# Quarter tiles for the key-value products, and one half of the values scaled by GpSimd instead of VectorE

## What is computed

```python
qkv = xf @ qkv_w.T + qkv_b                       # xf: B x N x C, N = 128*128 pixels, C = 64
qkv = qkv.reshape(B, N, HEADS, 3 * HEADC).transpose(0, 2, 1, 3)
q, k, v = jnp.split(qkv, 3, axis=-1)             # 8 heads of 8
k = _layernorm(k, kln_w, kln_b)                  # over the 8 of a head: (t - mean) / (std + eps)
v = _layernorm(v, vln_w, vln_b)
kv = jnp.einsum('bhnd,bhne->bhde', k, v) / N
av = jnp.einsum('bhnd,bhde->bhne', q, kv)
```

## Time and profile before

| | |
|---|---|
| median of 3 runs | 2723.24 us (2722.13 to 2723.75) |
| the profiled execution's own time | 2722.5 us |
| its span | 2720.6 us |
| TensorE busy, share of the span | 2563.4 us, 94% |
| VectorE | 1866.0 us, 69% |
| ScalarE | 1238.3 us, 46% |
| GpSimd | 159.3 us, 6% |
| share of the chain that ended last in the sweeps' products (L719) | 80% |
| key-value stage, first bias product to last Gram burst | 2456.35 to 2631.62 us |

### The profile page before, as it was taken

The page is one execution under the profiler, slowest core; times in us unless marked ns, Lnnn a source line. Parts: engine busy times, 40 slices in busy tenths (PEclk is TensorE's granted clock), DMA queues, the critical chain, the costliest instruction groups (busy, mean ns, idle before and its releaser), DMA issues.

```text
span 2720.6 us, 115694 instructions
## 1 busy us (share of the span) xinstructions
PE 2563.4 (94%) x45062; PEld 2447.6 (90%) x45062; DVE 1866.0 (69%) x6022; ACT 1238.3 (46%) x2502; POOL 159.3 (6%) x275
## 2 busy tenths in 40 slices
PE   2889999999999999997899999999999999959999
PEld 1279999999999999997899999999999999959973
DVE  7976666666566666678666666666666666777875
ACT  1656664222233333356666632222333334566768
POOL 1420000000000000000000000000000000003434
PEclk9999999999999999999899999999999999989989
DMA  6720001222400000023900012223000000240005
GB/s 259 179 73 0 0 0 32 62 60 60 104 0 0 0 5 0 0 62 103 373 22 0 0 39 62 61 60 96 0 0 0 0 0 0 77 108 2 3 14 235
DMA packets 158375, 146.46 MB, mean 54 GB/s; under 512 B 22497, under 2 KB 146018, under 8 KB 154210
## 3 DMA queue, kind: packets, MB, share of 16 engines
q1 hardware_dynamic: 146432, 142.65, 17.9%
q10 hardware_dynamic: 11874, 2.90, 0.5%
HBM read 61.61 MB, written 50.33 MB: 41 GB/s over the span
## 4 chain that ended last, share of the span: by engine, by line
PE 88%; DVE 3%; issue 3%; DMA 3%; ACT 2%; SPq 1%; ACTq 0%; POOL 0%; DVEq 0%
PE banks L719 80%; PE banks L773 4%; PE banks L785 1%; DVE state L915 1%; DMA state<-x_in 1%; PE banks L766 1%; ACT res L481 1%; PE banks L692 1%; DVE state L1023 1%; DMA res<-resid 1%; SPq L262 1%; DMA resid<-state 0%; ACT state L487 0%; POOL state L421 0%; DMA state<-turn_ring 0%
## 5 line engine op out<-in xcount | busy, mean ns | idle before, releaser
L719 PE MATMUL banks<-x_row,w_taps 128*64 128x124 f32 (+2 forms) x40640 | 2201.6, 270 | 14.4 <-DVE x_row L946 8.3
L719 PEld LDWEIGHTS banks<-x_row,w_taps 128*64 128x64 f32 x40640 | 2199.1, 135 | 16.7 <-DVE x_row L946 9.9
L946 DVE SCALAR_TENSOR_TENSOR x_row<-banks,sweep_nbias,biased_row 128x128 f32<-128x128 f32 x2032 | 713.2, 351 | 718.8 <-PE banks L719 702.9
L521 ACT ACTIVATE biased_row<-state,sweep_bias 128x256 f32 (+1 forms) x762 | 512.1, 673 | 1025.6 <-DVE state L949 589.2
L517 ACT ACTIVATE biased_row<-state,aff,gn_a 128x64 f32 (+1 forms) x1016 | 367.0, 432 | 179.3 <-DVE state L955 179.3
L949 DVE SCALAR_TENSOR_TENSOR state<-banks,sweep_nbias,biased_row 128x128 f32 (+1 forms) x1016 | 443.5, 437 | 0.1
L955 DVE SCALAR_TENSOR_TENSOR state<-banks,sweep_nbias,biased_row 128x64 f32 (+1 forms) x1016 | 237.2, 275 | 0.2
L955 DVE SCALAR_TENSOR_TENSOR turn_ring<-banks,sweep_nbias,biased_row 128x64 f32<-128x64 f32 x1016 | 237.3, 276 | 0.0
L407 POOL TENSOR_SCALAR res<-res 128x128 f32<-128x128 f32 x64 | 43.2, 675 | 2395.6 <-ACT res L630 2395.4
L692 PE MATMUL banks<-res,ffn_w 64*64 64x512 f32 x512 | 120.2, 611 | 11.6 <-DVE state L915 10.4
L773 PEld LDWEIGHTS banks<-kvw_s,state 64*128 64x128 f32 x1024 | 118.0, 308 | 0.1
(11 more groups left out here) (123 smaller groups left out, 780.4 us busy)
## 6 DMA issues: line engine op xcount, KB each, us to landing
state<-turn_ring SPq DMA_DIRECT2D x512, 64.0 KB, 1.9
state<-x_in SPq DMA_DIRECT2D x16, 1024.0 KB, 20.8
resid<-state SPq DMA_DIRECT2D x64, 256.0 KB, 3.7
res<-resid SPq DMA_DIRECT2D x16, 1024.0 KB, 8.9
res<-resid SPq DMA_DIRECT2D x32, 512.0 KB, 6.0
resid<-state SPq DMA_DIRECT2D x16, 1024.0 KB, 10.6
out_y<-state SPq DMA_DIRECT2D x16, 1024.0 KB, 3.9
state<-resid SPq DMA_DIRECT2D x32, 256.0 KB, 8.5
```

The source lines that it names most:

```text
L521: nc.scalar.activation(as_cells(n, biased_row[:, k, :, :]), cells(n, slice(0, B), i, k, g), ACT.Identity, bias=sweep_bias[:, n:n + 1]).the ...
L719: last = nc.tensor.matmul(out_ps[blk, :, lo:hi], w_taps[:, n % 2, s, blk], x_row[c][src][:, :, s + lo:s + hi], start=at == 0, stop=at == T ...
L946: nc.vector.scalar_tensor_tensor(x_row[c][par][:, :, 2:2 + HALF], ps, nb, br, ALU.max, ALU.add).then_inc(row_ready[c], 1)
```

## The change

Three things are changed, all in the key-value stage. The product of 128 pixels (weights of 128 columns) becomes two of 64 pixels, each to its half of the output partitions. VectorE's scaling takes only the four pixel groups of the even parity, 256 elements a partition. The four of the odd parity are scaled by GpSimd, in `scale_odd_pixels(n - 1)`, which stands behind `tails(n)`; the Gram product waits for both. Nothing is left out of the computation.

```diff
+        odd_v_scaled = sem("odd_v_scaled")
...
+        def values_and_scale(n, u):
+
+            by = rkv[:, n % KV_SLOTS, :].rearrange("p (u h) -> p u h", h=HEADS)[:, u, :]
+            return gram_kv[:, n % KV_SLOTS, u, 1, :, :], by.unsqueeze(3).to_broadcast([P, PARTS, HEADS, HD])
...
+            def scale_odd_pixels(n):
+
+                pool.wait_ge(inverse_ready, n + 1)
+                pool.wait_ge(kv_copied, n + 1)
+                v, by = values_and_scale(n, slice(PARTS, 2 * PARTS))
+                nc.gpsimd.tensor_tensor(v, v, by, ALU.mult).then_inc(odd_v_scaled, 1)
+
             for n in range(KV_TILES):
                 tails(n)
+                if n:
+                    scale_odd_pixels(n - 1)
+            scale_odd_pixels(KV_TILES - 1)
...
                         col = q * BANK + t * KVN
-                        last = nc.tensor.matmul(pair[n % KV_BANKS][:, col:col + KVN], half_rows[blk, top:top + P, b, w],
-                                                kvw_s[blk, b, :], start=False, stop=t == PARTS - 1)
+                        for m in range(2):
+                            at = slice(m * C, (m + 1) * C)
+                            last = nc.tensor.matmul(pair[n % KV_BANKS][at, col:col + KVN],
+                                                    half_rows[blk, top + m * C:top + (m + 1) * C, b, w],
+                                                    kvw_s[blk, b, :], start=False, stop=t == PARTS - 1)
                 last.then_inc(kv_done, 1)
...
                 pe.wait_ge(v_scaled, n + 1)
+                pe.wait_ge(odd_v_scaled, n + 1)
...
-                v = gram_kv[:, slot_, :, 1, :, :]
-                by = rkv[:, slot_, :].rearrange("p (u h) -> p u h", h=HEADS).unsqueeze(3).to_broadcast([P, 2 * PARTS, HEADS, HD])
+                v, by = values_and_scale(n, slice(0, PARTS))
                 nc.vector.tensor_tensor(v, v, by, ALU.mult).then_inc(v_scaled, 1)
```

## The result

The changed kernel takes **2700.53 us** (median of 4 runs, 2699.72 to 2701.83), the kernel before 2723.49 us in the same session (4 runs, 2722.13 to 2724.07). The ratio is 0.9917, 95% interval 0.9900 to 0.9934: 23 us faster. The forecast was 2694, its range 2679 to 2726. The profiled execution took 2700.32 us, its span is 2698.4 us, 22.2 less than before.

A forecast was written before the change was run, and what follows sets the result against it. TensorE was taken to bound the key-value stage at 2.677 us a tile; with GpSimd next at 2.13 + 0.05, 59 tiles save 29 us: 2722.5 becomes 2693.2, plus 0.7 for the median, 2694 us, range 2679 to 2726.

The forecast's parts named there:

- Part 1: Key-value products in quarter tiles: a group of four loads costs 0.11 us, eight 0.88, and TensorE's tile becomes 1.82 us.
- half-way case: Key-value loads partly take turns: 0.165 us a group, TensorE's tile 2.26, time 2699; counted within the forecast.
- Part 2: Next bound in the key-value stage: GpSimd at 2.13 us a tile, over VectorE's 1.91, TensorE's 1.82 and ScalarE's 1.79.
- P: Time of GpSimd's new scaling product of 256 elements, taken as 0.80 us; near 0.7 the sum would be below 35 us.
- Part 3: GpSimd's product and VectorE's scaling overlap: 0 to 0.27 us a tile, mostly in VectorE's spare 0.22; 0.05 taken.
- The new wait: The Gram products' wait for `odd_v_scaled` costs nothing as long as GpSimd's pace holds; about half a tile of slack.
- The start and the end as nothing: Before and behind the 59 tiles the change was taken as nothing: about 1 us each, of opposite sign.
- The loads take turns: Rival: strided loads of both column halves alternate, TensorE's tile stays at 2.70 us, time 2722 to 2726; chance 0.13.
- Exclusion: Rival: VectorE's 0.42 us scaling adds fully to GpSimd's tile, making 2.55; 7.5 us saved, 2716; chance 0.08.
- The clock: Rival: TensorE's clock falls to 1.2 GHz in the stage, tile near 3 us, 19 us slower, 2742; chance 0.03.
- P stayed far below 1.35: Rival: GpSimd's product is dear, deciding from 1.35 us; at 1.6 the kernel is 15 us slower, 2738; chance 0.06.
- The sum: Key-value stage: 2.677 - (2.13 + 0.05) = 0.50 us saved in each of 59 tiles, 29 us, 2693.2 profiled.

The follow-up runs named there:

- half_packed: Changed kernel, but the second column half's 64 weights are neighbouring elements of `state` (other pixels) while the first half stays strided; 2686.03 us.
- quarters_only: Changed kernel with the quarter products kept, but all scaling given back to VectorE and GpSimd's product and semaphore removed; 2699.02 us.
- packed_64: Changed kernel, quarters and split scaling kept, but each product's weights are 64 neighbouring elements of `state` (other pixels); 2686.82 us.
- packed_128_pool: Kernel before, with weights of 128 neighbouring elements of `state` (other pixels) and the scaling split between VectorE and GpSimd; 2683.31 us.

## Why the prediction was right and where it was off

**What bounds the kernel before: right.** TensorE's products set the stage's pace, and the gain came where it was looked for: 25.5 us in the 59 tiles on which the sum was made, less 3.3 ahead of them.

**Part 1, the group of four: the step that failed.** "If the two column halves read their weights side by side" a group was to be 0.11 us. It is 0.147 in the median (in one tile five groups in a row start at 2519.692, 2519.840, 2519.987, 2520.137 and 2520.288 in the single records, 0.149 apart): the rows of before showed a strided load beside a moving operand, and none showed two strided loads in one set of partitions. The argument that moving reads cost the loads nothing didn't carry over. half_packed shows the cost only where both are strided. So the products took 1.26 instead of 0.88, the first one stood 0.40 behind the bias product instead of 0.31, the Gram products took 0.58 instead of 0.63, and TensorE's tile was 2.24, not 1.82. The text had a half-way case, "0.165 a group, TensorE 2.26, 2699", and its time is what came, within 2 us. That it came so near is in part luck: with 0.147 a group the prediction's own terms give 0.63 + 0.31 + 1.18 = 2.12, below the 2.18 that it had for GpSimd. The other 0.12 are the 0.09 behind the bias product, which no row of before showed, and 0.08 by which the products take longer than eight groups, less 0.05 of the Gram products.

**Part 2, "GpSimd becomes the bound": wrong.** GpSimd idles in over 5 of 50 us in the changed kernel, and quarters_only has the same tile without its product. The estimate of its tile, 2.13, was too high as well: P was well placed as a sum (0.80 taken and 0.05 for the overlap; 0.83 to 0.89 measured in the means of the kernels, of which 0.63 are the product alone), but 0.16 for two more gaps and the 0.08 in the 1.33 were too much; three operations back to back have one gap of 0.09, 1.92 us in all. VectorE's 1.91 fits (packed_64's tile is 1.92 in the median, where TensorE has room), its scaling took 0.42 as in the earlier trace rows. By packed_64 and packed_128_pool, with products as short as Part 1 had them the time would have been near 2683 to 2687, not 2694: two errors of opposite sign, 0.42 us a tile too little for TensorE and over 0.2 too much for GpSimd, left the forecast only 6.5 us low. The number is near, then, but by luck and not by its mechanism: the engine that was named as the next bound was not the bound. (Its other sum, "below 35 us" with a P near 0.7, comes out at 35.2: 59 x (2.677 - 2.03 - 0.05).)

**Part 3, the overlap: right in kind, larger in size.** The product takes 0.63 alone and 0.83 to 0.89 with VectorE's scaling ahead of it, some 0.2 to 0.26 a tile instead of 0.05. In packed_128_pool and packed_64 it ends 0.91 us after the start of VectorE's scaling, whether it starts 0.045 us behind it (then it takes 0.867) or 0.092 (0.821): it loses what is left of the first 0.28 us of VectorE's 0.42, just as the prediction's 0.15 of free start would have it. What failed is the guess that GpSimd would lag: both are released by the reciprocal, and in 63 of 64 tiles GpSimd's product starts 0.04 to 0.12 us behind VectorE's. In the changed kernel it stays hidden below TensorE. The Trainium skill (SBUF — State Buffer, Who interferes with whom) has one engine blocked for the other's whole instruction; the trace agrees in part, for 0.28 of VectorE's 0.42 us. VectorE's own scaling stayed at 0.42, so "0.8 and more there" did not come.

**The new wait: right.** TensorE waits for L439 only at the stage's first tile (0.58 us at 2471.12) and its last ones. **The start and the end as nothing:** the end is the same within 0.04 us, the start cost 3.3 us. 1.7 of it stand ahead of all that was changed, and the first bias product starts between 2456.2 and 2460.4 in the kernels shown here. The 1.6 up to the first Gram burst go with a lower granted clock, 0.62 in the mean from 2458 to 2471 us: it is at half (1.2 GHz) until 2468.0 in the changed kernel and until 2459.9 before. Windows of the changed kernel:

```profile
2458.00:2471.00 13.00, 12.54 (x177) 9.64 (x176) 6.10 (x13) 7.24 (x11) 3.07 (x6) 0.62 0.01 1
```

and of the kernel before:

```profile
2456.00:2468.00 12.00, 11.27 (x109) 10.78 (x112) 6.38 (x14) 7.11 (x11) 2.60 (x5) 0.84 0.01 1
```

quarters_only, with the same loads, is at half until 2460.6 and takes 12.0 us there instead of 13.1. That it is the change's doing isn't shown.

**The rivals.** "The loads take turns" in full (0.22 a group) did not come, though a third of the way to it did. Exclusion came in part and was hidden. The clock was at 1.00 in the stage from 2468.0 to 2607.9 us, and P stayed far below 1.35. **The sum:** 59 x (2.677 - 2.245) = 25.5 stands for the 29.3 that were predicted, less the 3.3 of the start: 22.2 us. These 3.8 and 3.3 are the 7.1 us between the 2693.2 of the sum and the profiled 2700.3.

## What to carry to other kernels

Splitting a product over the quarters of the array pays when its weight loads set the pace; price a pair of loads in the same partitions by how they read, since packed weights here were worth as much alone (2700.6) as the quarters were (2699.0), and with the scaling split 17 us more (2683.3). Taking work off an engine that isn't the bound gives nothing, though it costs little: the same split of the scaling was worth 0 us under strided loads and 14 to 17 under packed ones, so measure it again when the bound has moved. Before multiplying small instructions, count what a tile must fetch: a burst can get shorter and the stage longer.

## What the runs showed of the hardware

- Loads of 128 columns with a step of 512 bytes come at half the pace of packed ones: pairs 0.220 and 0.112 us apart at full clock. The Trainium skill (SBUF — State Buffer, Door 1: The DMA port swizzle) has lines of 16 bytes, of which each wants at least two hits for full bandwidth. With a step of 512 bytes each line gets one, and the trace agrees that this is slower; the factor of two is the trace's, the page gives none.
- Two strided loads of 64 columns in one set of partitions slow each other: the groups come 0.147 us apart, where a strided load beside a packed one comes every 0.113 and packed quarters every 0.096. Beside such a pair ScalarE's copy went from 0.913 to 0.988 us and GpSimd's tail from 0.67 to 0.72. Laying the two streams 512 bytes apart instead of 32 KB changed none of it.
- GpSimd's product and VectorE's scaling, both with two inputs, overlapped for free only in the last 0.14 us of VectorE's 0.42: GpSimd's 0.63 became 0.87 when it started 0.045 us behind, and 0.82 when it started 0.092 behind.
- TensorE stopped again and again for instructions at one 16-KB fetch in 3.7 us (3.3 at the least), and a stage of many small products was slower for it (2734.7 us). packed_64 already lost 0.08 us a tile to it, at 26 fetches in 100 us.
- After products of 128 output rows, the first load of a quarter stood 0.40 us behind the bias product, with 0.21 us idle, in every kernel with quarters; with 128 columns it was 0.31. At the other end it is the reverse: the first Gram product starts 0.31 us behind the last key-value product before and 0.12 in the changed kernel (packed: 0.20 in packed_128_pool, some 0.08 in packed_64 where nothing holds the Gram product back). So this wait seems to have moved rather than been added; its cause was not tested.
